# A gated expert layer in split fp32: the weights' rounding moved from GpSimd to ScalarE and VectorE, half of h kept in its PSUM bank, new orders on the engines

## The chip, the cores and the metric

One core of one Trainium2 chip runs the whole program. The metric is the device time of one execution in microseconds. A matmul works on fp32r operands; each fp32 value is held as a rounded high part and a low part, and each product is the sum of three matmuls.

## The reference, cut to what matters

```python
g = einsum('bsd,edf->ebsf', x, Wg)            # E = 8 experts, B = 2, S = 1024, D = 256, F = 1024
u = einsum('bsd,edf->ebsf', x, Wu)
expert_outs = einsum('ebsf,efd->ebsd', silu(g) * u, Wd)
expert_output = einsum('be,ebsd->bsd', gating_probs, expert_outs)
shared = einsum('bsf,fd->bsd', silu(x @ Sg) * (x @ Su), Sd)
x = x + (1 - sg) * expert_output + sg * shared
# second layer: attention pooling with one of three masks per batch
scores = tanh(x @ W1 + b1) @ v
p = softmax(where(mask, scores, -1e30))       # mask: prefix, postfix or all but itself
x = x + (p @ x) / cnt
```

## The kernel before

The first layer carries nearly all of the time. A **use** is one block of 128 hidden units of one expert (or of the shared one): its columns of Wg and Wu and its rows of Wd. A **group** is one use for one batch (1024 tokens). Experts go in chunks of 4 uses, each chunk first for batch 0, then for batch 1: 8 groups for 4 uses, 128 groups for the eight experts. The shared expert follows with 8 groups for batch 0 and 8 for batch 1, and each of its blocks is a new use for each batch: 80 uses and 144 groups.

The products of a group (x times Wg, x times Wu, for two halves of 512 tokens and two halves of D) are made with seven products instead of eight, by Strassen's and Winograd's scheme. Sums of the quarters of x (`xs`, seven of them, made once per batch) meet sums of the quarters of the weights (`wq`, seven per use). Each product is three matmuls of 128x128 by 128x512 (`three_pass`: L902, L903, L904): high by high, low by high, high by low. So a group has 21 matmuls for `g` and `u`, and 12 in `down` (two output halves by two token halves by three), which add h times Wd of the group two places earlier (`LAG`) to the `acc` banks.

**Weights.** SP loads pairs of uses into two slots (`load_pair`, three DMAs), waiting for `d_split`, which frees the slot. GpSimd makes the sums in place (`combine`, L368, L370, L371, counted by `t_step`), then splits each use: `wq_hi` = rounded (L360), `wq_lo` = the rest (L363), `wd_hi` and `wd_lo` likewise (L377, L380). Six uses have room (`RING`); a split waits until the last reader of its slot is done.

**One group i.** TensorE runs `p4(i)`, `p5(i)`, `gate_start(i+1)` (product 1 into `g_ps`), `down(0, i-2)`, `gate_end(i+1)` (product 2 into `g_ps`), `p3(i)`, `p7(i+1)`, `p6(i+1)`, `down(1, i-2)`. Between products 1 and 2 ScalarE copies `g_ps` into `v_ps` (`seed`, L491), to which products 6, 5 and 3 are added. ScalarE's list for group i: silu of the second half's gate (`gate_second`, L515), `seed(i+1)`, rounding of the second half's h (`round_h(1, i)`, L521), silu of the first half (`gate_first(i+1)`, L497), copies of product 7 and of the unfinished `v_ps` (`keep_p7`, `keep_v`, L503, L509), `round_h(0, i)`. VectorE's list: `second_gate` (L701), `second_up` (L706), h of the second half (`hidden_second`, L713), `rest_h(1, i)` (L726: h minus its rounded part), additions of finished `acc` banks to x where they are due (`add_acc`, L735), h of the first half (`hidden_first`, L721), `rest_h(0, i)`. The two `v_ps` banks alternate by group. Orders are written out by hand; semaphores hold the engines together.

**The start.** x of both batches is transposed on TensorE into the `acc` banks; ScalarE copies it to `xT`; VectorE makes the sums of quarters (`combine_x`), and both engines split them (`round_x`, `rest_x`). For batch 1 the four sums fall behind `rest_h(1, 0)` in group 0, its splits into groups 1 and 2. `keep_busy` runs matmuls on zeros.

**The second layer.** From group 138 on (`L1_AT`) the products, copies and scans for batch 0 are spread between the last groups (`first_bank`, `second_bank`, `second_layer`); batch 1 follows behind group 143.

Of the kernel before, what the change touches and what calls it, by code (L numbers as in the profile page):

```python
# [6 lines left out]
F32 = mybir.dt.float32  # L7
F32R = mybir.dt.float32r
I32 = mybir.dt.int32
ALU = mybir.AluOpType  # L10
# [22 lines left out]
def cond_resid_kernel(nc, x, fside, shared_gate, prompt_type, Wg, Wu, Wd, Sg, Su, Sd, W1, b1, v, out):  # L33
# [22 lines left out]
    for e in range(E):  # L56
        for c in range(FT // CHUNK):
# [13 lines left out]
    first_of_b = [min(i for i, g in enumerate(groups) if g[0] == b) for b in range(B)]  # L71
    end_of_b = [max(i for i, g in enumerate(groups) if g[0] == b) for b in range(B)]
# [7 lines left out]
    with ExitStack() as ctx:  # L80
# [48 lines left out]
        h = [sb(f"h{t}", [P, BANK]) for t in range(NT)]  # L129
# [82 lines left out]
        xT_copied = sem("xT_copied")  # L212
        s_done = [sem(f"s_done{b}") for b in range(B)]
# [77 lines left out]

        def x_source(b, q):
            if q in SQ:
                return s_tmp[SQ[q]][:]
            t, k = {1: (0, 0), 2: (0, 1), 4: (1, 1)}[q]
            return xT[:, b, k, t * BANK:(t + 1) * BANK]

        block = ctx.enter_context(nc.Block())

        @block.sync  # L300
        def _(sp):
# [5 lines left out]
            def load_pair(m):  # L307
                e, f = uses[m * PAIR]
                g, u, d = (Wg[e], Wu[e], Wd[e]) if e < E else (Sg, Su, Sd)
                s, cols = m % RAWS, slice(f * P, (f + PAIR) * P)  # L310
                sp.dma_start(raw[:, s, 1:3, :],
                             g[:, cols].rearrange("(k p) f -> p k f", p=P)).then_inc(staged[s], 16)
                sp.dma_start(raw[:, s, 0:4:3, :],
                             u[:, cols].rearrange("(k p) f -> p k f", p=P)).then_inc(staged[s], 16)
                sp.dma_start(raw_d[:, s, :, :],
                             d[cols, :].rearrange("(j p) d -> p j d", p=P)).then_inc(staged[s], 16)

            load_x(0, 0)
            load_pair(0)
            load_x(0, 1)  # L320
            load_pair(1)
# [17 lines left out]
        def _(pool):  # L339
# [43 lines left out]
            def split_tile(n):  # L383
# [10 lines left out]
                else:  # L394
# [4 lines left out]
                    if n >= RING:  # L399
                        pool.wait_ge(p_done[3], final_group[n - RING] + 1)  # L400
# [724 lines left out]
```

## Time and profile before

| | us |
|---|---|
| median of 3 runs | 1250.21 |
| lowest, highest | 1246.8, 1250.62 |
| profiled execution | 1246.65 |
| its span, first to last instruction | 1244.9 |
| mean granted TensorE clock | 0.979 of full |

| engine | busy us | share of the span | instructions |
|---|---|---|---|
| TensorE matmul | 1167.8 | 94% | 4972 |
| TensorE weight load | 928.9 | 75% | 4972 |
| VectorE | 900.5 | 72% | 1104 |
| ScalarE | 620.4 | 50% | 1074 |
| GpSimd | 606.7 | 49% | 498 |

The DMA queues moved 36.67 MB, 29 GB/s over the span. Durations come from the one profiled execution; matmuls overlap, so a row's 0.39 us is not the distance between two of them. In the rows PE is TensorE, PEld its weight load, DVE VectorE, ACT ScalarE, POOL GpSimd, SP SyncE, and L12 is line 12 of the kernel. "[0.83 <-ACT v_ps L491]" says that the engine was idle for 0.83 us before the instruction, until ScalarE's L491 on `v_ps` was done.

### The profile page before, as it was taken

The numbers are of one execution on the slowest core, as the hardware profiler recorded it, in microseconds if no ns is written. First come the engines' busy times: TensorE is split into PE (matmuls) and PEld (weight loads), VectorE is DVE, ScalarE is ACT, GpSimd is POOL, SyncE is SP. The second block draws the span as 40 slices with busy tenths as digits, with TensorE's granted clock in tenths as the row PEclk, the third lists the DMA queues.
The fourth block names the chain that finished last, engine by engine and source line by source line (L and its number), as shares of the span: only waits on it lengthen the run. The fifth ranks groups of instructions, "written<-read, shape, count | busy, mean of one in ns | idle before, by whom it ended". The sixth has DMA issues, their size and how long they took to land. (4 is left out here: it accounts for less than half of the span.)

```text
span 1244.9 us, 14736 instructions
## 1 busy us (share of the span) xinstructions
PE 1167.8 (94%) x4972; PEld 928.9 (75%) x4972; DVE 900.5 (72%) x1104; ACT 620.4 (50%) x1074; POOL 606.7 (49%) x498
## 2 busy tenths in 40 slices
PE   7699999999999999999999999999999999999988
PEld 5477787878787777777777787878787878776645
DVE  5767677777777767676767676777777777887656
ACT  4354555555555455555555455555454545444532
POOL 6917172646464626263535344444444444899000
PEclk7799999999999999999999999999999999999988
DMA  4100000000000000000000000000000010110001
GB/s 144 44 11 26 26 26 26 26 26 26 26 26 26 26 26 26 27 26 26 26 26 26 26 26 26 26 26 26 26 26 26 17 35 4 49 51 26 1 9 60
DMA packets 37930, 36.67 MB, mean 29 GB/s; under 512 B 3040, under 2 KB 37856, under 8 KB 37856
## 3 DMA queue, kind: packets, MB, share of 16 engines
q1 hardware_dynamic: 37568, 35.73, 8.9%
q8 instruction: 40, 0.66, 0.2%
q14 instruction: 34, 0.28, 0.1%
q10 hardware_dynamic: 288, 0.01, 0.0%
HBM read 33.63 MB, written 2.10 MB: 29 GB/s over the span
## 5 line engine op out<-in xcount | busy, mean ns | idle before, releaser
L726 DVE TENSOR_TENSOR h_lo<-h,h_hi 128x512 fp32r<-128x512 f32 x288 | 314.0, 1090 | 252.0 <-ACT h_hi L521 252.0
L360 POOL TENSOR_TENSOR wq_hi<-raw,zero 128x896 fp32r<-128x896 f32 (+1 forms) x81 | 143.2, 1768 | 261.0 <-PE v_ps L904 251.3
L521 ACT ACTIVATE h_hi<-h 128x512 fp32r<-128x512 f32 x288 | 181.3, 629 | 171.7 <-DVE h L713 112.1
L515 ACT ACTIVATE silu<-gate 128x512 f32<-128x512 f32 x144 | 91.1, 633 | 270.4 <-DVE gate L701 270.4
L902 PE MATMUL acc<-h_hi,wd_hi 128*128 128x512 f32 x576 | 224.7, 390 | 0.0
L904 PE MATMUL acc<-h_lo,wd_hi 128*128 128x512 f32 x576 | 224.3, 389 | 0.0
L903 PE MATMUL acc<-h_hi,wd_lo 128*128 128x512 f32 x576 | 224.3, 389 | 0.0
L377 POOL TENSOR_TENSOR wd_hi<-raw_d,zero 128x256 fp32r<-128x256 f32 x80 | 65.9, 824 | 274.4 <-PE acc L904 274.3
L363 POOL TENSOR_TENSOR wq_lo<-raw,wq_hi 128x896 fp32r<-128x896 f32 (+1 forms) x81 | 185.6, 2291 | 6.3
L902 PE MATMUL g_ps<-xs_hi,wq_hi 128*128 128x512 f32 x288 | 119.8, 416 | 60.4 <-ACT v_ps L491 60.3
L713 DVE SCALAR_TENSOR_TENSOR h<-silu,gates,up 128x512 f32<-128x512 f32 x144 | 161.7, 1123 | 13.6
L902 PE MATMUL v_ps<-xs_hi,wq_hi 128*128 128x512 f32 x432 | 169.9, 393 | 0.0
L904 PE MATMUL v_ps<-xs_lo,wq_hi 128*128 128x512 f32 x432 | 169.9, 393 | 0.0
L903 PE MATMUL v_ps<-xs_hi,wq_lo 128*128 128x512 f32 x432 | 169.7, 393 | 0.0
L503 ACT ACTIVATE p_sb<-e_ps 128x512 f32<-128x512 f32 x144 | 86.1, 598 | 89.7 <-PE e_ps L904 89.7
L902 PEld LDWEIGHTS g_ps<-xs_hi,wq_hi 128*128 128x128 f32 x288 | 54.3, 189 | 95.6 <-ACT v_ps L491 84.9
L902 PEld LDWEIGHTS acc<-h_hi,wd_hi 128*128 128x128 f32 x576 | 108.3, 188 | 22.9 <-issue 0.4
L903 PEld LDWEIGHTS acc<-h_hi,wd_lo 128*128 128x128 f32 x576 | 108.3, 188 | 22.5
L904 PEld LDWEIGHTS acc<-h_lo,wd_hi 128*128 128x128 f32 x576 | 108.2, 188 | 22.5
L721 DVE SCALAR_TENSOR_TENSOR h<-silu,gates,v_ps 128x512 f32<-128x512 f32 x144 | 106.6, 740 | 18.8 <-PE v_ps L904 16.3
L902 PE MATMUL e_ps<-xs_hi,wq_hi 128*128 128x512 f32 x288 | 114.6, 398 | 2.4 <-ACT x L544 2.4
L701 DVE TENSOR_TENSOR gate<-e_ps,v_part 128x512 f32<-128x512 f32 x144 | 98.6, 685 | 22.4 <-PE e_ps L904 22.4
(144 smaller groups left out, 1833.4 us busy)
## 6 DMA issues: line engine op xcount, KB each, us to landing
raw<-in_L_cond_Wg SPq DMA_DIRECT2D x32, 256.0 KB, 2.7
raw<-in_L_cond_Wu SPq DMA_DIRECT2D x32, 256.0 KB, 3.2
raw_d<-in_L_cond_Wd SPq DMA_DIRECT2D x32, 256.0 KB, 3.7
x_nat<-in_x SPq DMA_DIRECT2D x8, 256.0 KB, 6.3
raw<-in_L_cond_Sg SPq DMA_DIRECT2D x8, 256.0 KB, 2.7
raw<-in_L_cond_Su SPq DMA_DIRECT2D x8, 256.0 KB, 3.0
raw_d<-in_L_cond_Sd SPq DMA_DIRECT2D x8, 256.0 KB, 3.6
out_x<-x_nat SPq DMA_DIRECT2D x8, 256.0 KB, 2.1
```

What stands on the lines that cost most here:

```text
L360: nc.gpsimd.tensor_tensor(hi, src, zero[:, 0:1].unsqueeze(2).broadcast_to([P, n, P]), ALU.add).then_inc(hi_done, 1)
L363: nc.gpsimd.tensor_tensor(lo, src, hi.bitcast(F32), ALU.subtract).then_inc(lo_done, 1)
L503: nc.scalar.activation(p7_sb[:], e_ps[:], ACT.Copy).then_inc(p7_copied, 1)
L515: nc.scalar.activation(silu1[:], gate1[:], ACT.Silu).then_inc(silu1_done, 1)
L521: nc.scalar.activation(h_hi[t][:, i % HB, :], h[t][:], ACT.Copy).then_inc(h_hi_done[t], 1)
L701: nc.vector.tensor_tensor(gate1[:], e_ps[:], v_part[:], ALU.add).then_inc(gate1_done, 1)
L713: nc.vector.scalar_tensor_tensor(out=h[1][:], in0=silu1[:], scalar=gate_of(i), in1=up1[:], op0=ALU.mult, op1=ALU.mult).then_inc(h_done[1], 1)
L721: nc.vector.scalar_tensor_tensor(out=h[0][:], in0=silu0[:, i % 2, :], scalar=gate_of(i), in1=v_ps[i % 2][:], op0=ALU.mult, op1=ALU.mult).t ...
L726: nc.vector.tensor_tensor(h_lo[t][:, i % HB, :], h[t][:], h_hi[t][:, i % HB, :].bitcast(F32), ALU.subtract).then_inc(h_split[t], 1)
L902: nc.tensor.matmul(ps, w_hi, a_hi, start=start, stop=False, skip_group_check=True)
L903: nc.tensor.matmul(ps, w_lo, a_hi, start=False, stop=False, skip_group_check=True)
L904: return nc.tensor.matmul(ps, w_hi, a_lo, start=False, stop=stop, skip_group_check=True)
```

## The change

- The rounding of the seven weight sums leaves GpSimd: ScalarE writes `wq_hi` (`round_w`), VectorE subtracts for `wq_lo` (`rest_w`), for all uses but the first. `round_at` says behind which group's list ScalarE does it; VectorE does it one group later, between `second_gate` and `second_up`. `round_w` waits for GpSimd's sums (`t_step`) and for the ring; SP's loads also wait for `gu_split`.
- The shared expert's blocks are split once where the ring still holds them: 10 uses instead of 16, 74 in all; batch 1 takes its blocks in another order.
- h of the first half is written over `v_ps` (`h_of`), and rounded and subtracted from there. `seed` waits for `h_split[0]`. One bank of `h` in SBUF is gone.
- Orders: TensorE runs `gate_start(i+1)` ahead of `p5(i)`. ScalarE: `seed(i+1)`, `gate_second(i)`, `gate_first(i+1)`, `round_h(1, i)`, bank copies of the second layer, `keep_p7(i+1)`, `round_h(0, i)`, `keep_v(i+1)`, `round_w`, x. VectorE: `second_gate`, `rest_w`, `second_up`, second layer, `add_acc(1)`, `hidden_second`, `add_acc(0)`, `hidden_first`, both `rest_h`, x.
- The start: x of batch 0 is loaded first by SP, pair 0 by ScalarE's queue. The parts of x of batch 0 are rounded and subtracted from the `acc` banks, VectorE copies one of them to `xT`, and the transposes of batch 1 wait for all seven. Its sums and splits are spread over groups 0 to 3. The gates are made last. `keep_busy` is 12 and 4 instead of 8 and 12.

```diff
+    n0 = len(uses)
+    for f in (*range(FT), *range(FT - RING)):
+        uses.append((E, f))
     for b in range(B):
         for f in range(FT):
-            uses.append((E, f))
-            groups.append((b, len(uses) - 1, f == 0, f == FT - 1))
+            groups.append((b, n0 + f + b * (FT - RING), f == 0, f == FT - 1))
+    round_at = {}
+    for n in range(2, NU):
+        at = n - 2
+        if n >= CHUNK:
+            at = max(first_group[n] - 7 + n % CHUNK, max(round_at) + 1)
+        if n >= RING:
+            at = max(at, final_group[n - RING])
+        assert at <= first_group[n] - 2 and at not in round_at
+        round_at[at] = n
...
+        def h_of(t, i):
+            return h1[:] if t else v_ps[i % 2][:]
...
-            load_x(0, 0)
-            load_pair(0)
-            load_x(0, 1)
-            load_pair(1)
+            for t in range(NT):
+                load_x(0, t)
+            load_pair(sp, 1)
...
                 sp.wait_ge(d_split, (m - RAWS + 1) * PAIR)
-                load_pair(m)
+                sp.wait_ge(gu_split, (m - RAWS + 1) * PAIR)
+                load_pair(sp, m)
...
-                    if n >= RING:
-                        pool.wait_ge(p_done[3], final_group[n - RING] + 1)
-                    elif n >= RING // 2:
-                        pool.wait_ge(xT_done, B * KD * NT)
-                    split(w[:, 1:8, :], hi, lo, NP, gu_hi_done, n + 1, gu_split)
                 split_d(n)
...
+            def round_w(n):
+                act.wait_ge(t_step, 3 * (n // PAIR + 2 if n >= PAIR else n + 1))
+                if n >= RING:
+                    act.wait_ge(p_done[3], final_group[n - RING] + 1)
+                elif n >= RING // 2:
+                    act.wait_ge(xT_done, B * KD * NT)
+                s, j = n // PAIR % RAWS, n % PAIR
+                nc.scalar.activation(weights(n)[0], raw[:, s, 1:8, j * P:(j + 1) * P], ACT.Copy).then_inc(gu_hi_done, 1)
...
             def seed(i):
                 act.wait_ge(p_done[1], i + 1)
                 if i >= 2:
-                    act.wait_ge(h_done[0], i - 1)
+                    act.wait_ge(h_split[0], i - 1)
...
             for i in range(NG):
+                if i + 1 < NG:
+                    seed(i + 1)
                 gate_second(i)
                 if i + 1 < NG:
-                    seed(i + 1)
+                    gate_first(i + 1)
                 round_h(1, i)
                 first_bank(i - L1_AT)
                 if i + 1 < NG:
-                    gate_first(i + 1)
                     keep_p7(i + 1)
+                round_h(0, i)
+                if i + 1 < NG:
                     keep_v(i + 1)
+                if i in round_at:
+                    round_w(round_at[i])
...
-                nc.vector.scalar_tensor_tensor(out=h[0][:], in0=silu0[:, i % 2, :], scalar=gate_of(i),
+                nc.vector.scalar_tensor_tensor(out=v_ps[i % 2][:], in0=silu0[:, i % 2, :], scalar=gate_of(i),
                                                in1=v_ps[i % 2][:], op0=ALU.mult, op1=ALU.mult).then_inc(h_done[0], 1)
...
             for i in range(NG):
                 second_gate(i)
+                if i - 1 in round_at:
+                    rest_w(round_at[i - 1])
                 second_up(i)
                 second_layer(i - L1_AT)
-                hidden_second(i)
                 if i > LAG and groups[i - LAG - 1][3]:
                     add_acc(1, i - LAG - 1)
-                rest_h(1, i)
+                hidden_second(i)
                 if i >= LAG and groups[i - LAG][3]:
                     add_acc(0, i - LAG)
+                hidden_first(i)
+                rest_h(1, i)
+                rest_h(0, i)
...
             p7(0)
             p6(0)
+            pe.wait_ge(xs_split[0], NP)
+            pe.wait_ge(xT_own, 1)
+            transpose_x(1, *range(NT))
             for i in range(NG):
                 p4(i)
-                p5(i)
                 if i + 1 < NG:
                     gate_start(i + 1)
+                p5(i)
```

## Rows read from the trace of the kernel before

**Rows 1.** windows: stretch, length, busy us (count) by engine, clock, DMA share, GB/s

```profile
0.00:28.58 28.58, 20.47 (x69) 15.55 (x70) 15.52 (x19) 11.25 (x19) 19.33 (x24) 0.76 0.39 131
28.58:107.11 78.53, 62.51 (x243) 48.98 (x242) 54.54 (x64) 36.65 (x63) 43.59 (x33) 0.89 0.09 31
107.11:1055.93 948.82, 912.44 (x3961) 741.54 (x3960) 698.10 (x841) 489.94 (x840) 449.00 (x373) 1.00 0.08 26
1055.93:1187.05 131.12, 123.60 (x523) 94.57 (x522) 98.00 (x105) 65.42 (x115) 88.89 (x68) 1.00 0.10 31
1187.05:1244.90 57.85, 48.82 (x182) 28.27 (x180) 34.31 (x79) 17.15 (x37) 5.91 (x3) 0.85 0.11 37
```

**Rows 2.** timeline of quiet groups: start us, duration us, engine, line, operation, [idle before]

```profile
510.39 0.58 ACT L491 ACTIVATE v_ps<-g_ps 128x512 f32<-128x512 f32 x1
511.55 0.39 PE L902 MATMUL g_ps<-xs_hi,wq_hi 128*128 128x512 f32 x1
...
571.70 0.69 DVE L726 TENSOR_TENSOR h_lo<-h,h_hi 128x512 fp32r<-128x512 f32 x1 [1.52 <-ACT h_hi L521]
...
572.59 0.69 DVE L701 TENSOR_TENSOR gate<-e_ps,v_part 128x512 f32<-128x512 f32 x1 [0.20 <-PE e_ps L904]
...
580.07 0.69 DVE L701 TENSOR_TENSOR gate<-e_ps,v_part 128x512 f32<-128x512 f32 x1 [0.20 <-PE e_ps L904]
```

**Rows 3.** waits of the whole span: total us, times, longest us

```profile
ACT silu L515 <- DVE gate L701: 270.4, 144, 3.3
DVE h_lo L726 <- ACT h_hi L521: 252.0, 255, 2.9
PE g_ps L902 <- ACT v_ps L491: 60.3, 55, 8.1
```

**Rows 4.** timeline of a late group

```profile
553.50 2.12 POOL L363 TENSOR_TENSOR wq_lo<-raw,wq_hi 128x896 fp32r<-128x896 f32 x1
553.57 2.60 DVE L726 TENSOR_TENSOR h_lo<-h,h_hi 128x512 fp32r<-128x512 f32 x1 [1.03 <-ACT h_hi L521]
...
557.34 0.58 ACT L491 ACTIVATE v_ps<-g_ps 128x512 f32<-128x512 f32 x1
...
557.97 0.50 PE L902 MATMUL g_ps<-xs_hi,wq_hi 128*128 128x512 f32 x1 [0.83 <-ACT v_ps L491]
```

**Rows 5.** instructions by form: shapes, count, busy us, mean ns, idle before

```profile
L726 DVE TENSOR_TENSOR h_lo<-h,h_hi 128x512 fp32r<-128x512 f32 x288 | 314.0, 1090 | 252.0 <-ACT h_hi L521 252.0
...
L363 POOL TENSOR_TENSOR wq_lo<-raw,wq_hi 128x896 fp32r<-128x896 f32 x79 | 182.9, 2315 | 6.2
...
L721 DVE SCALAR_TENSOR_TENSOR h<-silu,gates,v_ps 128x512 f32<-128x512 f32 x144 | 106.6, 740 | 18.8 <-PE v_ps L904 16.3
...
L735 DVE TENSOR_TENSOR xT<-acc,xT 128x512 f32<-128x512 f32 x136 | 87.0, 680 | 7.6 <-PE acc L904 7.5
...
L368 POOL TENSOR_TENSOR raw<-raw 128x512 f32<-128x512 f32 x39 | 52.0, 1334 | 0.3
...
L782 DVE TENSOR_TENSOR score_self<-mask,qmax 128x1024 f32<-128x1024 f32 x2 | 2.5, 1225 | 0.1
...
L559 ACT ACTIVATE carry<-carry,blk_max_col 8x1024 f32<-8x1024 f32 x2 | 2.3, 1132 | 0.0
```

**Rows 6.** timeline of the start, and one wait in the second layer

```profile
9.12 0.70 POOL L360 TENSOR_TENSOR wq_hi<-raw,zero 128x256 fp32r<-128x256 f32 x1 [7.72 <-DMA raw_d<-in_L_cond_Wd]
...
22.00 2.16 DVE L674 TENSOR_TENSOR xs_lo<-s_tmp,xs_hi 128x512 fp32r<-128x512 f32 x1
...
32.92 2.61 DVE L656 TENSOR_TENSOR s_tmp<-xT 128x512 f32<-128x512 f32 x1
...
44.05 0.79 PE L902 MATMUL g_ps<-xs_hi,wq_hi 128*128 128x512 f32 x1 [8.07 <-ACT v_ps L491]
...
57.58 0.80 PE L902 MATMUL g_ps<-xs_hi,wq_hi 128*128 128x512 f32 x1 [4.26 <-ACT v_ps L491]
...
1165.58 0.47 PE L902 MATMUL e_ps<-xs_hi,wq_hi 128*128 128x512 f32 x1 [1.38 <-ACT x L544]
```

More of the change, by code:

```diff
@@ L128, in cond_resid_kernel @@
         blank = place("blank", [P, BANK], F32R, cursor[0])
-        h = [sb(f"h{t}", [P, BANK]) for t in range(NT)]
+        h1 = sb("h1", [P, BANK])
         h_hi = [sb(f"h_hi{t}", [P, HB, BANK], F32R) for t in range(NT)]
@@ L587, in second_bank @@
                     copy_x1(0, 2 * (k - 2) + 1)
-            copy_xT(0)
-            for q in (7, 6, 4, 5, 3):
+            for q in (1, 2, 4):
                 round_x(0, q)
+                copy_xT(0, BLOCK[q])
+            round_x(0, 7)
             seed(0)
+            for q in (6, 5, 3):
+                round_x(0, q)
             gate_first(0)
-            copy_xT(1)
             keep_p7(0)
             keep_v(0)
+            round_w(1)
+            copy_xT(1, (0, 0), (0, 1), (1, 0), (1, 1))
+            ROUND_X1 = {1: (1, 2, 7), 2: (6, 4, 5), 3: (3,)}
             for i in range(NG):
+                if i + 1 < NG:
+                    seed(i + 1)
                 gate_second(i)
                 if i + 1 < NG:
-                    seed(i + 1)
+                    gate_first(i + 1)
                 round_h(1, i)
@@ L603, in _ @@
                 if i + 1 < NG:
[L604 removed]
                     keep_p7(i + 1)
+                round_h(0, i)
+                if i + 1 < NG:
                     keep_v(i + 1)
[L607 to L613 removed]
+                if i in round_at:
+                    round_w(round_at[i])
+                for q in ROUND_X1.get(i, ()):
+                    round_x(1, q)
                 second_bank(i - L1_AT)
@@ L685, in _ @@
             combine_x(0, 6)
+            rest_x(0, 7)
             combine_x(0, 3)
-            for n, q in enumerate((6, 4, 5, 3)):
-                rest_x(0, q, (xs_hi_done[0], n + 2))
-            dve.wait_ge(gate_step, 1 + 2 * B)
+            for q in (6, 4, 5, 3):
+                rest_x(0, q)
+            dve.wait_ge(gates_loaded, 2 * 16)
+            nc.vector.tensor_scalar(sg_rest[:], sg[:], -1.0, 1.0, ALU.mult, ALU.add).then_inc(gate_step, 1)
+            dve.wait_ge(gate_step, 1)
+            for b in range(B):
+                nc.vector.tensor_scalar(gates[:, b, 0:E], probs[:, b, :], sg_rest[:, b:b + 1], None,
+                                        ALU.mult).then_inc(gate_step, 1)
+                nc.vector.tensor_copy(gates[:, b, E:NEXP], sg[:, b:b + 1]).then_inc(gate_step, 1)
@@ new lines, in _, with rest_w @@
+            dve.wait_ge(gate_step, 1 + 2 * B)
+            COMBINE_X1 = {0: (7, 5), 1: (6, 3)}
+            REST_X1 = {1: (1, 2, 7), 2: (6, 4, 5), 3: (3,)}
+            def rest_w(n):
+                dve.wait_ge(gu_hi_done, n + 1)
+                hi, lo = weights(n)
+                s, j = n // PAIR % RAWS, n % PAIR
+                nc.vector.tensor_tensor(lo, raw[:, s, 1:8, j * P:(j + 1) * P], hi.bitcast(F32),
+                                        ALU.subtract).then_inc(gu_split, 1)
+            rest_w(1)
```

117 lines of the change are left out of this document (49 added, 68 removed).

## The prediction

> **What bounds the kernel now.** I read the stretches first, cut where VectorE starts the gate addition (`second_gate`) of groups 0, 8, 128 and 143 [rows 1]: 28.58 us until group 0, 78.53 us for groups 0 to 7, 948.82 us for groups 8 to 127, 131.12 us for 128 to 142, 57.85 us behind them. TensorE is busy for 96% of the third stretch at a granted clock of 1.00, and no other engine is above 74%: TensorE bounds the time, and what can be won is the time in which it waits.
>
> A quiet group lasts 580.07 - 572.59 = 7.48 us [rows 2]. It holds 33 matmuls (21 in seven products, 12 in `down`), so a product of three takes 0.68 us. Groups 0 and 1 have no `down` beside them: 21 / 33 x 7.48 = 4.76 us. Against that floor the stretches lose:
> - groups 0 to 7: 78.53 - (2 x 4.76 + 6 x 7.48) = 24.1 us
> - groups 8 to 127: 948.82 - 120 x 7.48 = 51.2 us, 3.4 in each period of 8 groups
> - groups 128 to 142: 131.12 - 15 x 7.48 = 18.9 us; I put about half of it to the same waits, the rest to TensorE's own added work for the second layer.
>
> The waits say for whom TensorE waits: 60.3 us in 55 places, all for the copy that seeds `v_ps` from `g_ps` (L491) [rows 3]. That copy stands behind the silu of the gate in ScalarE's queue, and this silu waits 270.4 us in all for VectorE's gate addition; VectorE waits 252.0 us for the rounding of h before `h_lo`. In a quiet group the seed ends at 510.97 and the product that needs it starts at 511.55 [rows 2]: 0.58 us to spare. In a late group [rows 4] VectorE's `h_lo` lasts 2.60 instead of about 0.69 us, since GpSimd's weight subtraction runs from 553.50 to 555.62; `h_lo` ends 0.55 us behind that. The gate addition of this group starts late, the seed only at 557.34, and TensorE has lost 0.83 us. So VectorE's operation with two SBUF inputs waits for GpSimd's running one, and the seed inherits the delay.
>
> By the Trainium skill ("SBUF — State Buffer", Who interferes with whom) a VectorE instruction with two SBUF inputs contends with a GpSimd instruction that reads SBUF, the later one blocks fully, and one with at most one SBUF input does not contend. The trace agrees: the delayed subtraction ends 0.55 us behind GpSimd's [rows 4], near the 0.53 us that 512 elements take at the slope of rows 5. The rule speaks for half of the change (h of the first half in PSUM) and against the other: the new weight subtraction on VectorE has two SBUF inputs. Priced by the lock, with every new subtraction that meets a combination behind its longest operation, the sum below would be 1201 us; without any contention, 1183.
>
> **The change, part by part.**
>
> *GpSimd loses the weight split.* 79 pairs of `wq_hi` and `wq_lo` (2.315 us for the second [rows 5]) go; it keeps the combinations (the longest of their three operations is 1.334 us [rows 5]) and the split of the down weights. VectorE's two-input operations have shorter ones to wait for. The mean of `h_lo` is 1.090 against 0.69 alone, 0.40 x 288 = 115 us of waiting [rows 2, 5].
>
> *Half the h stays in `v_ps`.* `hidden_first` writes over its PSUM input, and `rest_h(0)` has one SBUF input. The trace has no VectorE write to PSUM; its nearest rows are the same multiplication into SBUF at 0.740 and the gate addition out of PSUM at 0.69 [rows 2, 5], and I take 0.74 (0.6 to 0.9; it has 0.6 us of room either way). The bank is held longer: `seed(i+1)` now waits for `rest_h(0, i-1)`, the last of VectorE's list for group i-1. That ends, below, about 0.5 us into group i, and the seed must start by 2.7: cost nothing.
>
> *The new order.* TensorE's first product of group i+1 now stands ahead of `p5(i)`, so it is done 1.52 us into group i (0 is the start of `p4(i)`), and `seed(i+1)` stands ahead of the silu, waiting for no gate addition. The second product needs it at 3.40 us; the copy takes 0.58. Room grows from 0.58 to 1.2 us, and behind it stand no longer this group's VectorE steps but those of the group before. That takes away the cause of the 51.2 us.
>
> *What is late next: `p3(i)`.* It starts at 4.08 us and needs `second_up`, which now stands behind `p5` (done 2.20) and, in 74 groups, behind the new weight subtraction. That has 896 elements per partition; VectorE takes 0.69 for 512 and 1.225 for 1024 [rows 2, 5], so 1.09 by interpolation. VectorE in group i: gate 0.9 to 1.6; subtraction to 2.7; up to 3.35; room 0.7. Then the second half's product of h to 4.1, an accumulator add of 2 x 0.64 where due (0.680 each in their row, overlapping [rows 5]), the first half's to 6.1, the two `rest_h` to 7.7 or 8.1; the next gate addition can start at 8.4. ScalarE: seed 2.2, silu 2.8, silu of the first half 4.9, rounding 5.6, p7 copy 6.3, rounding 6.9, v copy 7.5, and `round_w`: 1.132 for 1024 [rows 5] scales to about 1.0 us, so 8.5 of the 9.0 at which the next seed is due. Two additions, two multiplications (0.740 each) and two subtractions (0.69 each [rows 2]) make 4.24 us per group; per 8 groups VectorE has 8 x 4.24 + 4 x 1.09 + 8 x 0.64 = 43 us of work in 59.8. It all fits; TensorE would not wait at all without GpSimd.
>
> With it: `round_at` puts the subtractions in groups 0, 2, 4 and 6 of each period. GpSimd's down split waits for the last `down` of its slot, which falls at the start of groups 0 and 2; a combination of three operations follows at about 1.7 us, just where the subtraction starts. If the subtraction is first, nothing is lost; if it comes behind the 1.334 us, up ends 1.3 later against 0.7 of room, 0.6 lost. Twice per period this is 0 to 1.2, over 15 periods 0 to 18 us. I take 9, since either order is as likely: **51.2 - 9 = 42 us gained** (33 to 51).
>
> *The start.* All of x of batch 0 is loaded ahead of pair 1, while ScalarE's queue issues pair 0; x is split from the banks; transposing batch 1 waits for VectorE's seven subtractions. GpSimd's first split starts at 9.12 [rows 6], which hardly moves. VectorE's list for batch 0 (about 5 of 11 operations with two SBUF inputs, 1.4 us each under a busy GpSimd, 0.7 the others) ends near 20 to 21 instead of 24.16 [rows 6], and the 16 transposes follow in some 3.6 (they ran ahead of that end before): group 0's gate addition comes at about 25, 3.5 us earlier. Groups 0 to 3: now VectorE combines batch 1 in one piece (the first of four operations takes 2.61), and TensorE waits 8.07 and 4.26 us; the matmul behind the first wait lasts 0.79 instead of 0.39, so the granted clock is at its lower level of 1.2 GHz [rows 2, 6]. After, the same 11 operations are spread over four groups, but 4 weight subtractions of 1.09 join, and those of n = 2 and 3 stand right between `p4(i)` and the first product of group i+1 (they fall in the group ahead of their use). VectorE has through groups 0 to 3: 4 x 4.24 + 4 x 1.09 + 11 x 1.2 and some 3 us of waits, 38 us; TensorE waits about 5 in group 1, 7 in group 2, 1 in group 3, and keeps the slow clock for some 3 us. That is 16 to 18 of the 24.1 us lost: 6.5 us gained. **Start: 10 us gained** (3 to 16).
>
> *Groups 128 on.* Six uses are not split again (74 instead of 80), 3 loads less. Of the 9 us that I put to the seed, about 4 stay, with a subtraction in four groups in a row: 5 gained. In 138 to 141 I see a loss: the second layer's bank copies on ScalarE (`first_bank`) come behind `gate_first` and the rounding, which waits for VectorE's scans. TensorE waits 1.38 us for such a copy now [rows 6]; this becomes some 0.7 more in two groups and about 1 in the group with the scores: 2.5 lost. **2.5 us gained** (-3 to 8).
>
> *The end* (57.85 us) has the same work in nearly the same order: 0 (-1 to 1). *SP's wait for `gu_split` besides `d_split`*: the loads behind it in SP's queue come up to a group later; the pair lands 3 us after issue and is needed some 3 groups on: nothing, and a stall of ScalarE in `round_w` (and every seed behind it) if that cover goes.
>
> **Sum.** 1244.9 - 42 - 10 - 2.5 = 1190.4 us of span. The profiled execution took 1246.65, 1.75 more than its span: 1192 us. The median before is 1250.21, 3.6 above the profiled execution; the lowest is 1246.8. I forecast 1192.
>
> **Rivals.**
> - *Nothing collides* (subtractions always ahead of GpSimd): 9 us less in the middle, a good start of 16 gives 1192 - 9 - 6 = 1177. For it: rows 2 show a stretch with no GpSimd in which every wait is gone.
> - *The lateness only moves.* VectorE and ScalarE are chained several times per group; if each of the two collisions per period costs its whole 1.3, and each of the two groups with an accumulator add 0.3 by a late v copy (`keep_v` now stands behind `round_h(0)`), that is 15 x 3.2 = 48 us. I price it at half, as ScalarE has over 1 us of room: 1192 - 9 + 24 = 1207, or 1214 with the worst start. For it: waits of 252.0 and 270.4 between the two engines [rows 3].
> - *Slower: the subtraction ahead of `second_up` becomes the bound.* A GpSimd combination has three operations in a row; if the subtraction waits for two of them (1.33 each at most, 2.2 together) it takes 3.3 us, up ends at 5.6 and `p3` is 1.5 late. In all 60 groups of the middle: 90 - 51.2 = 39 us lost, 12.5 gained elsewhere: 1246.65 + 26 = 1273. It decides from 2.9 us per subtraction on (60 x 1.1 = 51.2 + 12.5 and 3.7). Against it: the waiting VectorE operation got its turn right behind one GpSimd operation [rows 4], and half of these groups have no GpSimd work.
> - *Held back by weights* (SP, GpSimd and ScalarE in a ring of waits): each of 37 pairs 1 us late makes 37 us, 1229. Against it: margins of 3 groups, 3 us at the least (group 130).
>
> **How the numbers follow.** Forecast (1180 to 1204) 0.5; nothing collides 0.2; only moves 0.2; weights 0.05; slower or equal 0.05. The range of 8 in 10 takes in the bounds 1174 (51 and 16 gained) and 1218: 1174 to 1218. A measurement of this kernel can tell 0.3%, 3.7 us, from no change: faster 0.95, same 0.02, slower 0.03.
>
> **What would show it.** Right: distances of 7.48 us between gate additions for most of groups 8 to 127; `h_lo` split into a PSUM form near 0.69 and an SBUF form; TensorE's waits for L491's successor near zero; new waits, if any, of `v_ps` products for up; subtraction near 1.1 to 1.3 us; `wq_hi` on ScalarE near 1.0. Wrong: a period of 8 groups above 61.5 us; TensorE waiting more than 15 us in all for the seed; group 8 later than 103 us; a granted clock below 1.00 in the middle.

## The result and the profile of the changed kernel

The changed kernel takes 1181.9 us (median of four, 1178.8 to 1184.4); the ratio to the kernel before is 0.946, 95% interval 0.943 to 0.950. The forecast was 1192 us with a range of 1174 to 1218. The profiled execution is the 1184.42 us one; its span is 1182.6 us.

Its windows, cut at VectorE's gate addition of groups 0, 8, 128, 138 and 143 (columns as in [rows 1]):

```profile
0.00:21.83 21.83, 16.36 (x63) 12.06 (x63) 11.10 (x20) 11.41 (x21) 13.22 (x22) 0.92 0.54 172
21.83:93.31 71.48, 60.83 (x241) 47.65 (x242) 48.71 (x69) 40.08 (x70) 18.00 (x20) 0.93 0.11 34
93.31:990.90 897.59, 897.59 (x3961) 743.24 (x3960) 632.24 (x900) 508.42 (x900) 215.69 (x252) 1.00 0.09 27
990.90:1065.70 74.80, 74.80 (x331) 61.94 (x330) 51.51 (x72) 43.14 (x76) 17.87 (x18) 1.00 0.07 22
1065.70:1122.64 56.94, 49.71 (x194) 34.21 (x193) 29.52 (x39) 24.93 (x45) 2.73 (x5) 0.97 0.00 0
1122.64:1182.60 59.96, 52.29 (x182) 30.29 (x180) 34.62 (x78) 17.11 (x37) 5.91 (x3) 0.82 0.10 36
```

Groups 8 to 127, called the middle below, now take 897.59 us and TensorE is busy for all of it: 120 x 7.48 = 897.6, so none of them loses anything. GpSimd's busy time there fell from 449.00 [rows 1] to 215.69 us. Against [rows 1] the stretches gain 6.75 (up to group 0), 7.05 (groups 0 to 7) and 51.23 us (8 to 127); groups 128 to 142 take 74.80 + 56.94 = 131.74 instead of 131.12, and the end takes 2.1 more. Together 62.3, the difference of the spans.

TensorE's waits in the whole span (total us, times, longest):

```profile
PE g_ps L946 <- DVE wq_lo L736: 9.6, 2, 5.1
PE e_ps L946 <- ACT x L571: 3.8, 2, 2.1
PE e_ps L946 <- ACT score_self L561: 1.7, 1, 1.7
```

The 60.3 us for the seed [rows 3] are gone (0.7 us in one place is left). What stands first now is the start: TensorE waits twice for VectorE's new weight subtraction. The two others are waits for ScalarE's copies for the second layer. (One wait of 4.2 us behind group 143, not shown, is in the kernel before as well, with 5.6 us.)

The forms that answer to [rows 5] (shapes, count, busy us, mean ns, idle before):

```profile
L763 DVE SCALAR_TENSOR_TENSOR h<-silu,gates,up 128x512 f32<-128x512 f32 x144 | 112.9, 784 | 9.7
L769 DVE SCALAR_TENSOR_TENSOR v_ps<-silu,gates,v_ps 128x512 f32<-128x512 f32 x144 | 108.5, 753 | 83.4 <-PE v_ps L948 81.3 <-issue 0.4
L774 DVE TENSOR_TENSOR h_lo<-h,h_hi 128x512 fp32r<-128x512 f32 x144 | 100.0, 694 | 0.7
L774 DVE TENSOR_TENSOR h_lo<-v_ps,h_hi 128x512 fp32r<-128x512 f32 x144 | 99.7, 692 | 56.5 <-ACT h_hi L548 56.4
L736 DVE TENSOR_TENSOR wq_lo<-raw,wq_hi 128x896 fp32r<-128x896 f32 x73 | 81.4, 1115 | 0.1
L389 POOL TENSOR_TENSOR raw<-raw 128x512 f32<-128x512 f32 x36 | 72.6, 2015 | 14.6 <-DMA raw_d<-in_L_cond_Wd 14.3
L511 ACT ACTIVATE wq_hi<-raw 128x896 fp32r<-128x896 f32 x73 | 70.4, 964 | 0.8 <-POOL raw L392 0.8
```

`h_lo` lasts 0.69 us in either form, where its mean was 1.090. The price has moved to GpSimd: its combination of 512 elements grew from 1.334 to 2.015 us, and TensorE never waits in the middle. Group 72 shows how:

```profile
572.03 0.69 DVE L751 TENSOR_TENSOR gate<-e_ps,v_part 128x512 f32<-128x512 f32 x1 [0.91 <-PE e_ps L948]
...
572.08 0.74 POOL L401 TENSOR_TENSOR wd_lo<-raw_d,wd_hi 128x256 fp32r<-128x256 f32 x1
...
572.63 1.14 DVE L736 TENSOR_TENSOR wq_lo<-raw,wq_hi 128x896 fp32r<-128x896 f32 x1
...
572.78 2.14 POOL L389 TENSOR_TENSOR raw<-raw 128x512 f32<-128x512 f32 x1
...
573.70 0.68 DVE L756 TENSOR_TENSOR up<-v_ps,p_sb 128x512 f32<-128x512 f32 x1
...
575.23 0.39 PE L946 MATMUL v_ps<-xs_hi,wq_hi 128*128 128x512 f32 x1
...
579.50 0.69 DVE L751 TENSOR_TENSOR gate<-e_ps,v_part 128x512 f32<-128x512 f32 x1 [0.91 <-PE e_ps L948]
```

VectorE's subtraction is ready while GpSimd's short `wd_lo` runs (to 572.82); it comes next, in 1.14 instead of 1.08 us, and GpSimd's combination waits behind it. `second_up` ends at 574.38, 0.85 us before `p3` needs it. The gate addition, which was late in half of the groups of the middle before, waits 0.85 to 0.91 us for TensorE in each of them. Of the 60 subtractions in the middle 30 meet GpSimd's `wd_lo` like this one; the 30 others meet no GpSimd work and take 1.08 us.

Where time is still lost, first group 1 and then group 140:

```profile
32.14 0.80 PE L946 MATMUL g_ps<-xs_hi,wq_hi 128*128 128x512 f32 x1 [4.50 <-DVE wq_lo L736]
32.73 0.63 PE L947 MATMUL g_ps<-xs_hi,wq_lo 128*128 128x512 f32 x1
```

```profile
1097.62 0.58 ACT L571 ACTIVATE x<-e_ps 128x512 f32<-128x512 f32 x1
...
1098.34 0.47 PE L946 MATMUL e_ps<-xs_hi,wq_hi 128*128 128x512 f32 x1 [2.11 <-ACT x L571]
...
1099.63 0.63 PE L948 MATMUL v_ps<-xs_lo,wq_hi 128*128 128x512 f32 x1
```

A matmul of 0.63 instead of 0.39 us is one at the lower granted clock, 0.50 of full, as the window shows (clock third from the end):

```profile
1099.80:1102.40 2.60, 2.60 (x8) 2.02 (x7) 0.69 (x1) 1.09 (x3) 0.00 (x0) 0.50 0.00 0
```

Behind the wait of 4.50 us the clock is low at once; behind the 2.11 us it is low from 1.3 us later until 1102.6.

### The profile page after: what moved, and what is told of

It reads as the page before. It is cut to its first block, busy times and chain, and to the rows that moved or that the text cites. A ratio compares the mean times of both kernels' runs of the same rounds, so it can differ in the third digit from the quotient of the medians.

```text
span 1182.6 us, 14777 instructions
## 1 busy us (share of the span) xinstructions
PE 1151.6 (97%) x4968; PEld 929.4 (79%) x4968; DVE 807.7 (68%) x1176; ACT 645.1 (55%) x1148; POOL 273.4 (23%) x319
## 4 chain that ended last, share of the span: by engine, by line
PE 92%; DVE 1%; ACT 1%; issue 0%; DVEq 0%; ACTq 0%
PE acc L946 11%; PE acc L948 11%; PE acc L947 11%; PE v_ps L946 8%; PE v_ps L948 8%; PE v_ps L947 8%; PE e_ps L946 5%; PE g_ps L946 5%; PE e_ps L948 5%; PE e_ps L947 5%; PE g_ps L948 5%; PE g_ps L947 5%; PE acc L1058 1%; PE acc L1063 0%; PE v_ps L1048 0%
## 5 line engine op out<-in xcount | busy, mean ns | idle before, releaser
L398 POOL TENSOR_TENSOR wd_hi<-raw_d,zero 128x256 fp32r<-128x256 f32 x74 | 46.6, 629 | 785.4 <-PE acc L948 784.8
L524 ACT ACTIVATE silu<-g_ps 128x512 f32<-128x512 f32 x144 | 86.2, 598 | 230.9 <-PE g_ps L948 230.9
L518 ACT ACTIVATE v_ps<-g_ps 128x512 f32<-128x512 f32 x144 | 83.8, 582 | 203.0 <-PE g_ps L948 203.0
L769 DVE SCALAR_TENSOR_TENSOR v_ps<-silu,gates,v_ps 128x512 f32<-128x512 f32 x144 | 108.5, 753 | 83.4 <-PE v_ps L948 81.3
L774 DVE TENSOR_TENSOR h_lo<-v_ps,h_hi 128x512 fp32r<-128x512 f32 x144 | 99.7, 692 | 56.5 <-ACT h_hi L548 56.4
L756 DVE TENSOR_TENSOR up<-v_ps,p_sb 128x512 f32<-128x512 f32 x144 | 98.9, 687 | 55.5 <-PE v_ps L948 55.5
L763 DVE SCALAR_TENSOR_TENSOR h<-silu,gates,up 128x512 f32<-128x512 f32 x144 | 112.9, 784 | 9.7
L947 PE MATMUL g_ps<-xs_hi,wq_lo 128*128 128x512 f32 x288 | 113.0, 392 | 0.0
L948 PE MATMUL g_ps<-xs_lo,wq_hi 128*128 128x512 f32 x288 | 112.8, 392 | 0.0
L947 PE MATMUL e_ps<-xs_hi,wq_lo 128*128 128x512 f32 x288 | 112.2, 389 | 0.0
```

Source lines behind the costliest of these rows:

```text
L398: nc.gpsimd.tensor_tensor(wd_hi[:, n % RING, :], raw_d[:, s, j, :], zero[:, 0:1].broadcast_to([P, D]), ALU.add).then_inc(d_hi_done, 1)
L518: nc.scalar.activation(v_ps[i % 2][:], g_ps[:], ACT.Copy).then_inc(seeded, 1)
L524: nc.scalar.activation(silu0[:, i % 2, :], g_ps[:], ACT.Silu).then_inc(silu0_done, 1)
L756: nc.vector.tensor_tensor(up1[:], v_ps[i % 2][:], p7_sb[:], ALU.add).then_inc(up1_done, 1)
L763: nc.vector.scalar_tensor_tensor(out=h1[:], in0=silu1[:], scalar=gate_of(i), in1=up1[:], op0=ALU.mult, op1=ALU.mult).then_inc(h_done[1], 1)
L769: nc.vector.scalar_tensor_tensor(out=v_ps[i % 2][:], in0=silu0[:, i % 2, :], scalar=gate_of(i), in1=v_ps[i % 2][:], op0=ALU.mult, op1=ALU. ...
```

## The experiments

My theory was that the middle was lost to one link, the seed behind the silu that waits for the gate addition, and that the new orders cut it. The rivals were that GpSimd's work, which holds up VectorE's subtractions, did it, so that taking the rounding off GpSimd, and half the h out of SBUF, carry the gain; and that the subtraction ahead of `second_up` is a bound that was only just missed. Twelve runs: five on what carries the middle, three on what the two ends cost, four on the price of the subtraction. Ratios are to the kernel before, on the same chip, with the 95% interval; that of the change itself is 0.946 [0.943, 0.950].

### What carries the middle

**The kernel before, with the seed ahead of the silu, and nothing else.**

```diff
-                gate_second(i)
                 if i + 1 < NG:
                     seed(i + 1)
+                gate_second(i)
                 round_h(1, i)
```

> The kernel before with one edit: seed(i+1) ahead of gate_second(i) in ScalarE's list. Theory A and C: TensorE's waits for the seed in the middle fall from 36 us to under 12, but some move to p3 behind second_up: 1200 to 1225. Theory B: the lateness of VectorE stays and is only waited for elsewhere: 1240 to 1252.

1213.5 us, 0.975 [0.972, 0.977]. Its middle takes 920.47 us instead of 948.82 [rows 1], and its waits are:

```profile
PE g_ps L902 <- ACT v_ps L491: 14.3, 4, 5.6
PE v_ps L902 <- DVE up L706: 9.6, 20, 0.6
```

The swap of two lines on one engine brings 2.5 of the 5.4%, and 28.4 of the 51.2 us in the middle. The seed wait of the middle is gone (what is left is at the start), but 22.9 us stay there, 1.5 per 8 groups. `second_up` is late for `p3` in 20 groups of the whole span, 9.6 us, of which 13 groups and 6.4 us are in the middle; the rest is spread, and I didn't follow it.

**The changed kernel with the rounding of the weights back on GpSimd.** All orders, the start, the PSUM half of h and the 74 uses stay.

```diff
+                    split(w[:, 1:8, :], hi, lo, NP, gu_hi_done, n + 1, gu_split)
                 split_d(n)
...
-                if i in round_at:
-                    round_w(round_at[i])
...
-                if i - 1 in round_at:
-                    rest_w(round_at[i - 1])
...
```

> The changed kernel, but GpSimd again rounds and subtracts the weight sums (74 uses, four operations of about 2 us per pair more); the new orders, h in v_ps and the start stay. Theory A (the order gives the seed its room, fewer GpSimd operations only take lateness away that the room would mostly hide): 1184 to 1200 us, the middle stretch losing 0 to 1.2 us per 8 groups. Theory B (GpSimd's hold on the port was the cause): most of the 51 us of the middle comes back, 1220 to 1240. Theory C (only the order matters): 1180 to 1184, and the weight move bought nothing.

1185.9 us, 0.952 [0.950, 0.953]. **And the same with h of the first half in SBUF again too**, so that only orders, start and the 74 uses are new:

```diff
         def h_of(t, i):
-            return h1[:] if t else v_ps[i % 2][:]
+            return h1[:] if t else h0[:]
...
```

(`seed` then waits for `h_done[0]` again, and `hidden_first` writes to `h0` once the last h in it is split.)

> As e1_gp_split, and h of the first half goes back to a buffer in SBUF, so that both subtractions of h have two SBUF inputs: what is left of the change is the orders, the start and 74 uses. Theory A: 1186 to 1206, some more than e1_gp_split since VectorE waits for GpSimd in twice as many subtractions. Theory B: 1235 or more. Theory C: 1180 to 1185.

1188.6 us, 0.955 [0.953, 0.958]. The windows of groups 8 to 127, of the first and then of the second:

```profile
92.97:991.25 898.28, 898.19 (x3961) 743.32 (x3960) 629.32 (x840) 459.53 (x840) 433.56 (x372) 1.00 0.09 27
```

```profile
94.63:993.57 898.94, 898.88 (x3961) 742.43 (x3960) 677.42 (x840) 469.90 (x840) 454.97 (x372) 1.00 0.09 27
```

GpSimd is as busy as before (433.56 and 454.97 against 449.00 us), VectorE's `h_lo` is as slow as before in the second one, and yet the middle loses 0.7 and 1.3 us instead of 51.2:

```profile
L777 DVE TENSOR_TENSOR h_lo<-h,h_hi 128x512 fp32r<-128x512 f32 x288 | 302.9, 1061 | 39.5 <-ACT h_hi L554 37.0
```

VectorE is held up as before, and in the middle this costs 1.3 us once the seed no longer stands behind the gate addition. So the rival falls: the orders are enough for the middle, and with them in place the move of the rounding, which is most of the diff, is worth 0.7 us of it. Between the ratios of 0.952 and 0.946 lies 0.5%; their intervals (from 0.9503, and up to 0.9499) just miss each other. The rest of this difference is at the ends; the last stretch takes 62.5 us at a clock of 0.77 there, and nothing shows that GpSimd's work lowers it. Not run was the kernel before with the rounding moved and the orders left: the relief alone may have won back a part of the middle too.

**Only h of the first half in SBUF again** (the last edit without the one before it, so with GpSimd relieved).

> The changed kernel with only h of the first half back in SBUF; ScalarE and VectorE keep the weights. Theory A: 1180 to 1187, as GpSimd has little left to hold VectorE up with and 0.8 us of room stand ahead of p3. Rival (the bank is what removed the waits): above 1195.

1185.0 us, 0.951 [0.949, 0.953]; its middle is 897.60 us, the same to 0.01. The bank is worth nothing there, and the intervals of the ratios overlap.

**TensorE's p5 ahead of gate_start again.**

```diff
                 p4(i)
+                p5(i)
                 if i + 1 < NG:
                     gate_start(i + 1)
-                p5(i)
```

> The changed kernel with TensorE running p5(i) ahead of gate_start(i+1), as the kernel before does; the seed still stands ahead of the silu on ScalarE. Theory (what counts is that the seed no longer stands behind the gate addition; its room shrinks to 0.6 us and is kept, while up gains 0.7 us): the middle stays at 7.48 us per group, 1176 to 1186 us. Rival (the room of 1.2 us is needed, since ScalarE reaches the seed late behind the v copy and the rounding of the weights): waits for the seed in half of the groups, 1190 us or more.

1178.3 us, 0.947 [0.943, 0.950]: no difference by the ratio, and again 897.60 us in the middle. The seed's 1.26 us of room were not needed; in this run it has 0.58 in each group of the middle. So of the orders it is ScalarE's and VectorE's that count, at least with the rounding off GpSimd. (Groups 138 to 142 take 52.59 instead of 56.94 us here; I didn't follow that.)

### What the two ends cost

**ScalarE's copies for the second layer ahead of the silu of the first half.**

```diff
                 gate_second(i)
+                first_bank(i - L1_AT)
                 if i + 1 < NG:
                     gate_first(i + 1)
                 round_h(1, i)
-                first_bank(i - L1_AT)
```

> The changed kernel with first_bank ahead of gate_first and round_h(1) in ScalarE's list (it acts in four groups, 138 to 141, alone). The trace shows TensorE waiting 1.17, 1.67, 2.11 and 1.67 us for these copies, and half the clock for some 3 us behind one. Theory: 5 to 9 us gained, 1173 to 1177. Rival (the second layer's scans on VectorE bound these groups): within 1 us of the changed kernel.

1172.3 us, 0.943 [0.940, 0.945]; the interval overlaps that of the change by 0.25%, the windows don't leave a doubt. Those of groups 138 to 142 and of the end are:

```profile
1066.92:1114.67 47.75, 47.12 (x194) 33.35 (x193) 29.52 (x39) 25.05 (x45) 2.73 (x5) 1.00 0.00 1
1114.67:1170.60 55.93, 48.28 (x182) 28.05 (x180) 34.35 (x78) 17.11 (x37) 5.91 (x3) 0.88 0.11 38
```

47.75 instead of 56.94 us: the four waits for the copies (1.17, 1.67, 2.11 and 1.67 us) are gone, and with them the stretch of low clock behind the 2.11 us. Three other runs with the same waits have no such stretch and take 55.28 to 55.35 us (the one with only h in SBUF again, and two that follow: the early subtractions, and the very last run). So the place of `first_bank` costs 7.5 us by its waits, and 9.2 where a low clock comes on top. This is a loss that the change itself brings: the kernel before needs 47.46 us for these five groups.

The end takes 55.93 instead of 59.96 us, at a clock of 0.88 instead of 0.82, and has no edit in it. It isn't the waits ahead of it that decide this. The run with the orders only has the same waits, and its groups 138 to 142 and its end are:

```profile
1068.70:1125.62 56.92, 49.66 (x194) 34.31 (x193) 28.59 (x38) 25.08 (x45) 6.49 (x7) 0.97 0.00 1
1125.62:1180.60 54.98, 46.94 (x182) 27.70 (x180) 34.41 (x78) 17.15 (x37) 5.91 (x3) 0.91 0.11 39
```

Over all the kernels with the new orders the end lasts 55.0 to 62.7 us at clocks of 0.93 to 0.77, with the same code in it.

**The weight subtractions of uses 2 and 3 at the end of groups 0 and 1**, ahead of the sums of x, instead of between `second_gate` and `second_up` of groups 1 and 2.

```diff
-                if i - 1 in round_at:
+                if i - 1 in round_at and i > 2:
                     rest_w(round_at[i - 1])
...
                 rest_h(0, i)
+                if i < 2:
+                    rest_w(round_at[i])
```

> The changed kernel with the weight subtractions of uses 2 and 3 at the end of groups 0 and 1, ahead of the sums of x of batch 1, instead of behind the gate addition of groups 1 and 2. TensorE waits 4.50 and 5.05 us for them now, while VectorE then sits idle for 3 us waiting for p5. Theory: the waits go, VectorE's own work bounds these groups: 4 to 8 us gained. Rival (VectorE's work is the bound already): within 1.5 us.

1178.5 us, 0.947 [0.945, 0.949]. Group 8 comes at 87.90 instead of 93.31 us and the wait shrinks by half:

```profile
PE g_ps L948 <- DVE wq_lo L736: 4.8, 2, 2.9
```

By the spans of the profiled executions the run gains 6.8 us (1175.8 against 1182.6; 5.4 of it by group 8, 1.6 by the missing stretch of low clock in groups 138 to 142), by the medians 3.4, below what I expected; by the ratios to the kernel before nothing is to be seen. This run alone settles nothing; the next does.

**Both.**

> The changed kernel with the two edits of the runs before together: ScalarE's bank copies of the second layer ahead of the silu of the first half, and the weight subtractions of uses 2 and 3 at the end of groups 0 and 1. Theory (the losses at the start and in groups 138 to 142 are two separate waits): the gains add up. The first edit alone gave 1172.3 with group 8 at 94.5 us, the second alone put group 8 at 87.9: 1164 to 1170 us. Rival (one loss feeds on the other, or the clock takes one of them back): 1171 or more.

1165.7 us (1165.4 to 1166.0), 0.936 [0.935, 0.938]: 1.0% better than the change by the ratios, 16.2 us by the medians, the best version here. Against the run with the copies alone (0.943) it is 0.6% better, with intervals apart: so the early subtractions are worth some 7 us. The windows that differ from the change:

```profile
23.36:87.88 64.52, 58.55 (x241) 45.41 (x240) 49.00 (x69) 39.71 (x69) 17.41 (x19) 0.97 0.12 37
...
1060.28:1108.05 47.77, 47.14 (x194) 33.35 (x193) 29.52 (x40) 25.08 (x45) 2.73 (x5) 1.00 0.00 1
1108.05:1164.00 55.95, 46.81 (x182) 26.52 (x180) 34.27 (x78) 17.12 (x37) 5.91 (x3) 0.93 0.11 38
```

In the profiled executions: 5.4 less by group 8, 9.2 in groups 138 to 142, 4.0 at the end: 18.6 of span. By the windows the two losses are separate, and the gains add up; the 4.0 at the end, and 1.6 of the 9.2, are a clock that other runs have without either edit.

### The price of the subtraction

**One added subtraction of 840 elements ahead of each weight subtraction** from use 4 on, written to a scratch tile. It doubles what stands ahead of `second_up`.

```diff
+        scratch = [sb(f"scratch{k}", [P, NP, 120], F32R) for k in range(1)]
         h_hi = [sb(f"h_hi{t}", [P, HB, BANK], F32R) for t in range(NT)]
...
+                for k in range(1 if n > 3 else 0):
...
+                    nc.vector.tensor_tensor(scratch[0][:], raw[:, s, 1:8, j * P:j * P + 120],
+                                            hi.bitcast(F32)[:, :, 0:120], ALU.subtract).then_inc(extra_done, 1)
                 nc.vector.tensor_tensor(lo, raw[:, s, 1:8, j * P:(j + 1) * P], hi.bitcast(F32),
```

> The changed kernel with an added subtraction of 840 elements per partition (into a scratch buffer) ahead of each weight subtraction from use 4 on: about 2.1 us of VectorE work where 1.1 stood, 70 times. In the trace second_up ends 0.85 us ahead of p3 in such a group. Theory A (p3 is what is late next, from 0.85 us of added work on): 0.2 to 0.5 us each, 1192 to 1215 with collisions. Rival (VectorE has room elsewhere, 28% idle): 1180 to 1185.

1251.2 us, 1.005 [1.003, 1.007]: the whole gain is gone, far above what I expected. **Two added subtractions**, by the same edit with

```diff
-                for k in range(1 if n > 3 else 0):
+                for k in range(2 if n > 3 else 0):
```

> As e5_sub2 with two added subtractions one after the other, about 3.1 us in all: the price that the slower rival of the prediction put on the weight subtraction. Theory A: 1.2 to 1.4 us in each of 70 groups, 84 to 98 us: 1265 to 1280, slower than before the change. Rival: under 1200.

1369.1 us, 1.100 [1.097, 1.102], a miss of 89 us. Two things stood in the traces that I had not priced. First, groups with no added operation lasted 7.61 us instead of 7.48. That led to the next run.

**The changed kernel with 32 unused bytes per partition ahead of h_hi.** The scratch tile of 3360 bytes (52.5 times 64) stood in the same place. No instruction differs from the changed kernel.

```diff
+        pad = sb("pad", [P, 8])
         h_hi = [sb(f"h_hi{t}", [P, HB, BANK], F32R) for t in range(NT)]
```

> The changed kernel with an unused tile of 32 bytes per partition ahead of h_hi, so that h_hi, h_lo and all small tiles behind them stand 32 bytes further on; no instruction is added. It asks why, with one added subtraction per use (whose scratch tile of 3360 bytes stood in the same place, 32 bytes more than a multiple of 64), even groups without any subtraction lasted 7.61 instead of 7.48 us. Theory (the place of h in SBUF slows the matmuls that read it): 7.61 us per group without any wait, 144 x 0.13 = 18 us more, 1197 to 1204 us. Rival (the added operations did it, or the size of the program): 7.48 us per group, 1178 to 1185 us.

1203.2 us, 0.965 [0.963, 0.968]: 21 us more by the medians for 32 bytes, 16.0 of them in the middle. The window of groups 8 to 127 and the matmuls that read h, then the same row of the changed kernel:

```profile
94.73:1008.33 913.60, 913.60 (x3961) 743.47 (x3960) 631.60 (x900) 510.31 (x900) 215.57 (x252) 1.00 0.08 27
...
L947 PE MATMUL acc<-h_hi,wd_hi 128*128 128x512 f32 x576 | 229.7, 399 | 0.0
```

```profile
L946 PE MATMUL acc<-h_hi,wd_hi 128*128 128x512 f32 x576 | 224.8, 390 | 0.0
```

913.60 / 120 = 7.61 us per group, with TensorE busy throughout and the clock at 1.00. So the slow groups are a matter of where `h_hi` and the tiles behind it stand, not of a wait. It isn't any shift: the run with h of the first half in SBUF has one bank, 2048 bytes, in the same place, and its middle is 897.60 us.

**The kernel with one added subtraction, its scratch tile behind all others**, so that h stands where the changed kernel has it.

```diff
-        scratch = [sb(f"scratch{k}", [P, NP, 120], F32R) for k in range(1)]
         h_hi = [sb(f"h_hi{t}", [P, HB, BANK], F32R) for t in range(NT)]
...
         rden = sb("rden", [P, B, NJ])
+        scratch = [sb(f"scratch{k}", [P, NP, 120], F32R) for k in range(1)]
```

> The kernel with one added subtraction of 840 elements ahead of each weight subtraction, with its scratch tile behind all other tiles, so that h stands where the changed kernel has it. It gave 1251.2 us with the tile ahead of h, where I expected 1192 to 1215; its trace has groups of 7.61 us and groups of 8.90 us where GpSimd's combination got in between the two subtractions. Theory (18 us of the miss are the place of h; the rest is the collision, 1.3 us in 30 groups): groups of 7.48, of 7.6 to 7.8 with a lone subtraction and near 8.8 with GpSimd, 1226 to 1238 us. Rival (the place of h is nothing and the operations themselves cost it all): 1245 to 1255 us.

1238.2 us, 0.994 [0.992, 0.996]: 13 us less for the same work, 10.6 of them in the middle, where I had put 18 to the place of h; the time is 0.2 us above the range that I expected. Its wait, and group 72, to be held beside that of the changed kernel above:

```profile
PE v_ps L953 <- DVE up L763: 34.0, 31, 2.0
```

```profile
597.21 0.74 POOL L403 TENSOR_TENSOR wd_lo<-raw_d,wd_hi 128x256 fp32r<-128x256 f32 x1
...
597.76 1.08 DVE L741 TENSOR_TENSOR scratch<-raw,wq_hi 128x840 fp32r<-128x840 f32 x1
...
597.91 2.08 POOL L391 TENSOR_TENSOR raw<-raw 128x512 f32<-128x512 f32 x1
...
598.76 2.17 DVE L743 TENSOR_TENSOR wq_lo<-raw,wq_hi 128x896 fp32r<-128x896 f32 x1
...
600.06 1.46 POOL L393 TENSOR_TENSOR raw<-raw 128x256 f32<-128x256 f32 x1
...
601.59 0.50 PE L953 MATMUL v_ps<-xs_hi,wq_hi 128*128 128x512 f32 x1 [1.07 <-DVE up L763]
```

That is the second thing. Both engines queue up, and they get their turn one operation each: VectorE's first, GpSimd's combination (from 598.84 to 599.99, though its row counts 2.08), then VectorE's second, which ends 0.94 us behind that and is charged 2.17. Ahead of `second_up` stand 3.17 us instead of 1.14, and `p3` is 1.07 late. In the gate additions of groups 8 to 127, 60 intervals are 7.48 us, 34 are 7.7 to 7.8 (two subtractions, no GpSimd, 2.0 us together) and 26 are near 8.85. They add up to 941.9 - 897.6 = 44.3 us, 35.7 of it in the 26 (each 1.07 of wait and 0.3 until the matmuls follow each other as before). The trace agrees with the Trainium skill ("SBUF — State Buffer", Who interferes with whom) that the later operation blocks fully, and adds which comes next.

With two added ones the waits for up in groups 8 to 127 are 96.2 us, but these groups lose more, 1054.79 - 913.6 = 141 us. A good part of the rest is in the matmuls behind a wait of 2.47 us:

```profile
664.28 0.80 PE L953 MATMUL v_ps<-xs_hi,wq_hi 128*128 128x512 f32 x1 [2.47 <-DVE up L763]
664.87 0.63 PE L954 MATMUL v_ps<-xs_hi,wq_lo 128*128 128x512 f32 x1
```

They start 0.43 us apart instead of 0.23 until 667.0, some 1.3 us more: here the granted clock went down after the wait. That is so behind 18 of the 26 waits of 2.5 us; behind the 8 others the clock stays up. An estimate from these figures: 18 x 1.3 = 23 us for the clock, and 0.3 us behind each of the 60 waits, 18 us, make 41 of the 45 us.

## Why the prediction was right, point by point

**The cause in the middle: right, and shown.** The seed's link to the gate addition was the loss. The kernel before with that swap alone gains nearly half of all, and the orders without the relief of GpSimd bring the middle to 898.9 us, where 897.6 is the floor. In the prediction I gave the relief of GpSimd and the PSUM half their own paragraphs without a price each; with the new orders in place they are worth 1.3 us in the middle.

**The size in the middle: 51.2 instead of 42.** The step that failed is "I take 9, since either order is as likely". There was one order only: in the 30 groups of the middle in which the two meet, `wd_lo` of GpSimd is running when the subtraction comes up, and the waiting VectorE operation is next, each time. That the turn is taken one operation each was in the row I cited against the slower rival [rows 4]; I didn't apply it to this term. Room before `p3` was given as 0.7 and is 0.85; the subtraction as 1.09 and is 1.115; the PSUM write as 0.74 and is 0.753; `round_w` as 1.0 and is 0.964.

**The start: 13.8 instead of 10.** The waits were close: 5, 7 and 1 us forecast in groups 1, 2 and 3, and 4.5, 5.05 and 1.03 measured; groups 0 to 7 gain 7.05 against 6.5. Group 0 comes 6.75 us earlier, not 3.5, at 21.83 instead of "about 25". I took no part of the start away by itself, so how much of that is the order of the loads and how much x out of the banks is open.

**Groups 128 on: 0.6 lost instead of 2.5 gained.** Two terms were off, in opposite ways. "5 gained" was too small: up to 137 no group loses anything, and groups 128 to 137 gain 8.9 us (83.7 before, 74.8 now). The step "2.5 lost" for `first_bank` behind `gate_first` and the rounding was the right place and sign, and four times too small: 9.5 us (56.94 against 47.46; some of it may be an offset at group 138, whose gate addition ran behind TensorE before). I priced the copy's own lateness (0.7, 0.7 and 1); measured were waits of 1.17, 1.67, 2.11 and 1.67 us where the kernel before has less, since the silu and a rounding that waits for VectorE's scans both stand ahead, and behind the 2.11 us a stretch of low clock. Moving one line gives it back. Some 1.6 us of the 9.5 are the low clock, which other runs with the same waits don't have.

**The tail: 2.1 lost instead of 0.** The work is the same; the clock is 0.82 instead of 0.85. The waits of 138 to 142 don't decide it: the end takes 54.98 us at 0.91 in the run with the orders only and 55.9 at 0.89 in the one with 32 unused bytes, which have them all, and 55.93 at 0.88 in the one that has none. Why the clock differs there from one profiled execution to the next stays open.

The errors were of both signs: +9.2 and +3.8 against -3.1 and -2.1, 7.8 us in sum, and 1184.4 for the profiled execution against 1192. That the total came this near is in part luck. One bound of the range was added up wrongly: 51 and 16 us gained make 1177 by the prediction's own sum, as in its first rival, and not 1174.

**The rivals.** "Nothing collides" at 1177 was the best one, and its mechanism is what happened in the middle; its start of 16 us gained came to 13.8, and the rest of what it misses (1184.4 against 1177) is behind group 128. "The lateness only moves": nothing of it, the gate addition waits for TensorE in every group of the middle. "Held back by weights": no wait for it. "The subtraction becomes the bound": its price was right. It said that the loss is what the subtraction lasts beyond 1.8 us (0.7 of room on 1.09). At 2.0 us in 34 groups and 3.17 in 26 this makes 42 us; 44.3 were measured, and that kernel lies 0.6% below the kernel before. It would decide from a mean of about 2.6 to 2.7 us, where I wrote 2.9. My expectations of the first two runs with added subtractions then left out GpSimd's operation between two of VectorE's, the place of h, and the clock.

The changed kernel's four times lie in two pairs, 1178.8 and 1179.6, and 1184.2 and 1184.4, at mean clocks of 0.989 and 0.984 to 0.985. Only one of the four was traced. Among kernels with the same code in a stretch the middle takes 897.60 us each time, group 8 comes at 93.31 or 94.52, and the end varies by up to 8 us with its clock, so the end is the likeliest place of the 5 us; that isn't shown.

## What to carry to other kernels

When the bounding engine waits for a chain that crosses two others within one iteration, put the step that it waits for ahead of the ones that wait, in their queues, before moving work off a contended engine: here two swapped lines brought nearly half of the gain and the orders nearly all of the middle, with VectorE held up by GpSimd as it was. A step on the way to a deadline is priced by the turns ahead of it, one operation of the other engine for each of one's own, so one long operation is safe where two short ones are not. And a rarely run piece (the second layer's copies) must be looked at again when the orders around it change; its five groups lost 7.5 to 9.2 us that one line gives back.

## What the runs showed of the hardware that I had not expected

- 32 bytes: with h 32 bytes further on in each partition, a group of 33 matmuls lasts 7.61 instead of 7.48 us, 1.8%, at a full clock and without a wait. The 12 matmuls that read h follow each other at 0.234 instead of 0.227 us, which is 0.08 of the 0.13; the rest is spread over the others. With 2048 bytes instead of 32 a group lasts 7.48 us. Why, and what other offsets do, was not tried.
- When an operation of GpSimd or VectorE that holds the other one up ends, the one that waits is next: VectorE's subtraction in 1.14 and GpSimd's combination in 2.14 us in one group, VectorE's second one in 2.17 in another.
- Behind waits of 2.1 to 2.5 us TensorE's matmuls can fall to 0.63 us for some 3 us, at a granted clock of 0.50: behind 18 of 26 waits of 2.5 us in one run, and behind the one of 2.11 us in the changed kernel, but not behind the same wait of 2.11 us in the run with the early subtractions. Behind a wait of 1.07 us one is at 0.50 and the next back at 0.40.
- ScalarE writes 896 rounded elements per partition in 0.964 us (mean of 73), VectorE subtracts as many in 1.08.
